# Laying every engine's order of steps anew in a one-core attention and feed-forward kernel

## The reference

```python
x = x + attn(layernorm(x), Wqkv, Wo)      # 16 heads of 32, causal mask, softmax over 512 keys
x = x + ffn(layernorm(x), w1, w3, w2)     # hidden width 1365
# attn: qkv = x @ Wqkv ; a = softmax(q k^T / sqrt(32)) ; o = (a @ v) @ Wo
# ffn:  each weight w is made ternary first: s = mean|w| ; w = clip(round(w / s), -1, 1) * s
#       (silu(x w1^T) * (x w3^T)) @ w2^T
```

## Time and profile before

| | |
|---|---|
| median of 3 runs | 579.03 us (578.77 to 580.35) |
| the profiled execution's own time | 580.78 us |
| its span, first to last instruction | 579.0 us |
| PE, DVE, POOL, ACT busy | 508.0, 411.8, 368.4, 330.2 us |
| mean granted TensorE clock | 0.941 |

### The profile page before, as it was taken

The page is one execution under the profiler, slowest core; times in us unless marked ns, Lnnn a source line. Parts: engine busy times, 40 slices in busy tenths (PEclk is TensorE's granted clock), DMA queues, the critical chain, the costliest instruction groups (busy, mean ns, idle before and its releaser), DMA issues.

```text
span 579.0 us, 11497 instructions
## 1 busy us (share of the span) xinstructions
PE 508.0 (88%) x4092; PEld 237.9 (41%) x4092; DVE 411.8 (71%) x1026; ACT 330.2 (57%) x833; POOL 368.4 (64%) x460
## 2 busy tenths in 40 slices
PE   2669754857999999999999999999999998839997
PEld 2224322333445444544444444454444454314443
DVE  6599787697899877966888879578878771523421
ACT  4769866777756875645467875363666752012320
POOL 3077689777968976776667887556668782312320
PEclk9689955878999999999999999999999999869999
DMA  8939978999889756387596565675783548030001
GB/s 312 316 30 278 193 170 160 252 200 211 153 141 162 145 124 131 56 158 194 108 167 143 90 131 97 141 180 114 101 173 75 109 87 208 9 63 1 0 37 72
DMA packets 224205, 79.52 MB, mean 137 GB/s; under 512 B 213226, under 2 KB 213226, under 8 KB 224148
## 3 DMA queue, kind: packets, MB, share of 16 engines
q1 hardware_dynamic: 224148, 78.79, 65.0%
HBM read 20.97 MB, written 4.19 MB: 43 GB/s over the span
## 4 chain that ended last, share of the span: by engine, by line
PE 69%; POOL 9%; DMA 8%; SPq 5%; DVE 4%; issue 2%; ACT 2%; DVEq 0%; ACTq 0%
PE work L1120 46%; PE work L1280 13%; DMA early<-early 4%; PE work L1239 4%; PE score_bank L1197 4%; POOL early L654 4%; PE work L1210 2%; DMA rows<-in_L_attn_x 2%; POOL late L687 2%; POOL early L687 1%; SPq L517 1%; DVE early L986 1%; DMA w_ternary<-early 1%; POOL rows L669 1%; DMA late<-rows 1%
## 5 line engine op out<-in xcount | busy, mean ns | idle before, releaser
L654 POOL TENSOR_TENSOR early<-early 128x512 f16<-128x512 f32 (+1 forms) x192 | 193.7, 1021 | 40.4 <-DVE early L986 26.5
L762 ACT ACTIVATE early<-early,exp_bias 128x512 f32<-128x512 f32 (+3 forms) x256 | 140.8, 551 | 76.7 <-POOL exp_bias L661 76.5
L1120 PE MATMUL work<-late,w_ternary 128*128 128x512 f16 (+1 forms) x704 | 158.9, 384 | 10.3 <-DMA late<-rows 10.3
L974 DVE CUSTOM_DVE_ANT_0 early<-score_bank,mask,scalars 128x512 f32<-128x512 f32 (+3 forms) x256 | 131.7, 543 | 32.7 <-POOL early L654 20.4
L986 DVE CAST early<-early 128x512 f16<-128x512 f32 (+1 forms) x148 | 99.5, 690 | 18.1 <-ACT early L762 14.7
L1120 PEld LDWEIGHTS work<-late,w_ternary 128*128 128x128 f16 (+1 forms) x704 | 69.2, 101 | 93.9 <-issue 17.9
L1120 PE MATMUL work<-xt,wqkv_hi 128*128 128x512 f16 x256 | 80.7, 398 | 2.9 <-DVE wqkv_lo L936 2.0
L1280 PE MATMUL work<-w_ternary,late 128*128 128x512 f16 (+1 forms) x352 | 77.7, 379 | 0.0
L679 POOL TENSOR_TENSOR late<-late 128x512 f16<-128x512 f32 (+1 forms) x44 | 51.3, 1168 | 40.1 <-ACT late L799 39.4
L792 ACT ACTIVATE late<-work,scalars 128x512 f32<-128x512 f32 (+1 forms) x44 | 30.0, 682 | 53.0 <-DVE late L1027 36.1
L1120 PE MATMUL work<-xt,wqkv_lo 128*128 128x512 f16 x128 | 51.0, 398 | 0.0
(11 more groups left out here) (103 smaller groups left out, 702.4 us busy)
## 6 DMA issues: line engine op xcount, KB each, us to landing
rows<-in_L_attn_x SPq DMA_DIRECT2D x16, 256.0 KB, 3.0
x_res<-in_L_attn_x SPq DMA_DIRECT2D x12, 256.0 KB, 3.2
out_y<-x_res SPq DMA_DIRECT2D x12, 256.0 KB, 2.8
late<-in_L_ffn_w SPq DMA_DIRECT2D x4, 682.5 KB, 5.5
early<-in_L_ffn_w SPq DMA_DIRECT2D x3, 768.0 KB, 12.8
late<-in_L_ffn_w SPq DMA_DIRECT2D x3, 768.0 KB, 6.7
late<-in_L_attn_Wqkv SPq DMA_DIRECT2D x4, 512.0 KB, 7.2
late<-in_L_attn_Wqkv SPq DMA_DIRECT2D x1, 1024.0 KB, 9.8
```

Source lines behind the costliest of these rows:

```text
L654: pool.tensor_tensor(split_view(s, p, 1, h), raw_view(s, p, h), split_view(s, p, 0, h), ALU.subtract).then_inc(low_done, 1)
L762: last = act.activation(piece, piece, ACT.Exp, bias=bias, accum_out=sums[:, s % 2, at:at + 1])
L974: last = dve.tensor_tensor_reduce(raws[n % RAWS][:, off:off + cols], score_bank[h][:, off:off + cols], mask[:, S - cols:S], scalar(exp_sca ...
L1120: last = pe.matmul(bank, lhs, rhs, start=(n == 0), stop=(n == len(terms) - 1))
```

## The change

The five lists of `ORDERS` are replaced by others. The same steps stand in them, none is added or dropped. Some pieces (the second line of a pair is after):

```diff
-sp:   x_load:1,1 res_load:0,2 res_load:0,1 x_load:1,0 weight_turn:w1,0 res_load:0,0 weight_turn:w1,1
+sp:   x_load:1,0 weight_load:w3,0 x_load:1,1 weight_turn:w1,0-2 weight_load:w3,1-3 probs_turn:0,0-2 xt:1,0-1
...
-pool: stats_x:0,0-3 weight_round:w1,0-6 stats_x:1,0 weight_round:w1,7-8 bias:0,0,1 weight_round:w1,9-10 low:0,0,0
+pool: stats_x:0,0-3 stats_x:1,0 weight_round:w1,0-6 bias:0,0,1 weight_round:w1,7 xt:1,0 weight_round:w1,8
+      bias:0,0,3 low:0,0,0-1 weight_round:w1,9-10 bias:0,1,1 low:0,0,2-3 stats_x:1,1 bias:0,1,3 low:0,1,0-2
...
-act:  weight_sum:w1,2 split:2 weight_sum:w1,3 split:3 split:8 split:4 k:0 q:0 weight_ternary:w1,0 split:5
+act:  weight_sum:w1,2 q:0 split:3 weight_sum:w1,3 norm_x:1,0 k:0 split:8 split:4 q:1 weight_ternary:w1,0 xt:1,0
+      weight_ternary:w1,1 split:5 weight_ternary:w1,2 k:1 weight_ternary:w1,3 exp:0,0,0 split:6-7 exp:0,0,1
...
-dve:  max:1,1,0-2 stats_x:1,2 max:1,1,3 high:1,1,0-1 stats_x:1,3 weight_mean:w3 high:1,1,2-3 max:1,2,0-1 values:0
+dve:  high:1,0,0 wo_split high:1,0,1 max:1,1,0 high:1,0,2 max:1,1,1 high:1,0,3 q:2 max:1,1,2 high:1,1,0 max:1,1,3
+      high:1,1,1 stats_x:1,2 max:1,2,0 high:1,1,2 max:1,2,1 high:1,1,3 stats_x:1,3 max:1,2,2 k:2 max:1,2,3
...
-pe:   scores:1,0 k:2 q:3 scores:1,1 inverse:0 weight_mean:w3 values:0 scores:1,2 scores:2,0-1 inverse:1
+pe:   scores:1,0 weight_mean:w3 q:2 inverse:0 q:3 scores:1,1 k:3 values:0 scores:1,2 k:2 scores:2,0-1 inverse:1
```

In code one wait changes. The DMA that turns a tile of the next batch's rows overwrites `xt`. Before, it waited for `q` and `k` of the batch's last slot and for the four `v`. Now it waits, for each of the four banks, for the last `q`, `k` or `v` of the batch that used that bank, which covers all twelve readers:

```diff
                 if kind == "xt":
-                    for used in [(m, GROUPS * b - 1) for m in "qk"] + [("v", b - 1, j) for j in range(ST)]:
-                        full(sp, used)
+                    readers = [(m, GROUPS * (b - 1) + g) for m in "qk" for g in range(GROUPS)]
+                    readers += [("v", b - 1, j) for j in range(ST)]
+                    for n_bank in range(NW):
+                        full(sp, max((r for r in readers if bank_of(r) == n_bank), key=turn_of))
                     sp.wait_ge(rows_split[n], ST * (b - 1) + i + 1)
```

312 lines of the change are left out of this document (159 added, 153 removed).

## The result

The changed kernel takes **611.65 us** (median of 4 runs, 611.0 to 612.59) against 579.69 of the kernel before on the same chip: ratio 1.056, interval 1.054 to 1.058. Slower was forecast, at 593.5 with a range to 605; the time lies outside it. The profiled execution has a span of 610.0 us against 579.0.

A forecast was written before the change was run, and what follows sets the result against it. PE's own work was taken to bound the kernel from 163 us on, softmax waits before it. Waits of +20.5 less 6 recovered gave +14.5: 595.3 profiled, 593.5 median; own range 587 to 600, with rivals 581 to 605.

The forecast's parts named there:

- First part: the x tile: At the start, DVE waits for the x tile behind Wo; q:0 7.8 us later, POOL's first w1 rounding +6.0 us.
- Second part: w3's load ahead of w1's turns: On SP, the w3 load waits for split:7 with w1's turns queued behind; the first fills' turns land +11.1 us later.
- Third part: the wait for all readers: Row turns wait for late k:2, so DVE stands 10.5 us for the third tile; 9.4 of +20.5 us.
- The clock: Idle PE falls to 1.2 GHz, so q:3, k:3 and k:2 take 5.1 us each; sum some 4 us higher.
- Recovery up to 163 us: Up to 163 us, early w3 rounds on POOL and a w3 turn out of the chain give back 6 us.
- The region from 163 us on, put at nothing: From 163 us on, PE's work is unchanged and others have room: no cost, 1 to 3 us if cover fails.
- PE gapless from about 178: Sign expected in the profile after; the sum is wrong if PE's gapless part starts within 5 us of 163.
- The sum: Whole kernel: 20.5 - 6 = +14.5 us, giving 595.3 profiled and 593.5 as median; chance 0.50.
- no recovery: Rival: slots up to 163 us run no tighter than before; +20.5 to 24.5 us, about 601; chance 0.20.

The follow-up runs named there:

- e1: Kernel after with stats_x:1,0 (the wait for the second batch's x tile) moved behind split:2 on DVE; 603.75 us, ratio to before 1.044.
- e2: Kernel after with w3's first load on SP moved between the second and third of w1's turns; 609.45 us, ratio 1.052.
- e3d: e3c plus weight_load:w2,0 ahead of the row turns and the statistics and norms of tiles 1,2 and 1,3 later still; 611.6 us, ratio 1.056.
- e3: Kernel after with k:2 alone moved directly behind q:2 on PE, ACT and DVE; 611.88 us, ratio 1.057.
- f1: Kernel before with all its old lists and only the new condition, row turns waiting for the last reader of every bank; 578.41 us, ratio 0.999.
- e8: Kernel after with the first probability turn of slots 1 and 2 moving only a quarter of its blocks (output not the reference's); 604.88 us, ratio 1.044.
- e5: Kernel after with the four w2 turns behind probs_turn:4,1 and v:1,3's drain ahead of high:5,0,0; 616.15 us, ratio 1.063.
- e5c: Kernel after with only w2's last turn behind probs_turn:4,1, probs_turn:4,2 ahead of the y turns, and v:1,3's drain earlier; 613.01 us, ratio 1.058.
- e6: Kernel after with the edits of e1, e2, e3b and e5 together; 609.14 us, ratio 1.051.
- e7: Kernel after with the edits of e1, e2, e3c and e5c together; 601.16 us, ratio 1.038.
- e10: Kernel after with the edits of e9 and e5c together; 618.3 us, ratio 1.067.
- e11: Kernel after with the edits of e1, e2, e3d, e9 and e5c together; 608.88 us, ratio 1.051.
- e12: Kernel after with w3's turns, the roundings and ternary steps of w2,1 to w2,3, ot:3 and v:1,3's drain earlier; 613.24 us, ratio 1.058.
- e3b: Kernel after with all four late projections of the first batch, with their drains, moved to where the kernel before has them; 614.21 us, ratio 1.060.
- e3c: Kernel after with probs_turn:1,0 ahead of the two row turns on SP, statistics and norms of tiles 1,2 and 1,3 later; 609.16 us, ratio 1.052.
- e9: Kernel after with w3's last rounding and turns, w2's last load, sums, mean, roundings and ternary steps all earlier; 615.45 us, ratio 1.062.
- g1: Kernel before with stats_x:1,0 moved behind k:0 on DVE; 575.37 us, ratio 0.992.

## Why the prediction was wrong, step by step

**First part: the x tile.** Right. `q:0` at 28.2 (forecast 28.8), first rounding at 37.1 (38.3), so +4.8 where +6.0 stood. By e1 the wait is worth 6.8 us at `values:0` and 7.9 in the time, the largest gain of a single reordering.

**Second part: w3's load ahead of w1's turns.** Right in kind. SP was silent until 50.3 (52), and the three turns were issued by 60.0 (third out at 59.1). `high:1,0,0` stood at 81.1 (80.6). By e2 the load's place is worth 3.4 us at `values:0` and 2.2 in the time.

**Third part: the wait for all readers.** The times were right: `k:2` at 93.0 to 95.8 (done 96.0), DVE idle 8.2 us (10.5) up to 101.9 (102.7), `probs_turn:1,0` at 100.9 (101), `high:1,2,0` at 110.0 (109), so +21.4 for the forecast +20.5. What the part is worth by itself was given as 9.4. The stretch `values:0` to `values:1` did lose 9.2, and e3d got 5.3 of it back. The other 4 were not isolated: e3 had nearly as short a stretch (27.5) only because `values:0` itself came 6.3 later. The wait without the lists costs nothing (f1).

**The clock.** The granted clock did fall where PE idled: from 100 to 163 us, with PE busy 34.2 of 63 us, it was 0.70 on average, against 0.88 with 50.2 of 63 before. The Trainium skill, "TensorE: Matmul & The Clock Gate", Part 1, says that an idle array falls to 1.2 GHz; the trace agrees with the rule. The price of 4 us, which I worked out for that rival, was wrong: `q:3`, `k:3` and `k:2` took 2.7 us each, at the high level. `q:2` stood ahead of them (76.6 to 81.3, 4.7 us, for the most part at the low level), PE was busy from 74.7 after 6.9 us of idle time, and from 70 to 100 the mean was 0.82, higher than before's 0.57.

**Recovery up to 163 us.** This step failed. I took -6: 4.2 us for w3's rounds done ahead on POOL and 2.3 for a turn of w3 out of the way, with DVE's 18 us of idle time as the room. Measured from `values:1` to `values:3`: -1.3. The old and the new lists take 45.0 to 46.9 us there in all thirteen kernels whose lists are unchanged from `values:1` to `values:3`. The rounds were done ahead, the sixth at 93.8 us, though by four and not six: by its own `high:1,2,0` at 88.54 the kernel before had started two (84.84 and 87.90). But a round less on POOL shortens nothing unless POOL is what the others wait for, and in the new lists DVE waited 8.4 us there for turned probabilities; e8 shows that shorter turns do shorten the slots. How much of the missing recovery this makes was not isolated. And the turn of w3 was not saved, only moved. SP of the kernel after:

```profile
122.20 3.20 SPq L611 DMA_TRANSPOSE w_ternary<-late  x1
...
165.49 4.20 SPq L611 DMA_TRANSPOSE w_ternary<-late  x2
```

One of the three still stands ahead of `probs_turn:2,0`. The other two stand just ahead of `values:3`, and ACT waited 3.25 us for them at 173.4, with `ot:3` behind it, for which PE idled 1.3 us ahead of `project:0,0`. An engine's idle time in such a stretch is not room until one knows what it waits for.

**The region from 163 us on, put at nothing.** This step failed by more: +10.5 us from `values:3` to `gate:0,0`. I argued that PE has no gaps from 163 on, so that only the point at which this begins could move, and granted 1 to 3 us if the cover failed. But that was a reading of the kernel before; in the new lists the stretch up to `gate:0,0` has gaps of its own (1.3 us ahead of the first projection, 7.7 ahead of `values:4`). "PE gapless from about 178" was the mark set for it, and it is gapless only from 208.6. SP of the kernel before in this place:

```profile
167.69 4.47 SPq L557 DMA_TRANSPOSE late<-rows  x2
172.25 1.92 SPq L568 DMA_TRANSPOSE early<-early  x1
175.25 2.60 SPq L557 DMA_TRANSPOSE late<-rows  x2
```

There the turns of y rows 0 and 1 left in one piece ahead of `probs_turn:4,2`, the second of them 23.7 us behind `values:3`. In the kernel after `probs_turn:4,2` stands between them, behind w2's four turns (8.1 us), and the second leaves at 201.8, 33.5 us behind `values:3`. What hangs on it can be followed in the rows. DVE, kernel after, then PE of e5:

```profile
205.18 1.16 DVE L891 TENSOR_SCALAR rows<-x_res,y_mean_var,y_rstd 128x512 f32<-128x512 f32 x1 [0.45 <-DMA late<-rows]
```

```profile
215.02 10.23 PE L1129 MATMUL work<-late,w_ternary 128*128 128x512 f16 x37 [1.35 <-DMA late<-rows]
```

DVE normalises y row 3 as soon as the turn of y row 1 has landed, ACT halves it by 207.0, its own turn leaves at 208.3 (behind `x_load:2,2` at 206.5 and y row 2's turn) and lands at 211.4, and `gate:0,0` needs it. In the kernel after PE comes to `gate:0,0` 1.2 us later than that, at 212.6, since `values:4` was late as well. So two chains of nearly the same length lead to this step, and mending `values:4` alone could give no more than about 1 us. In e5, e5c, e6, e7, e10, e11 and e12, where `v:1,3` stands earlier, the gate product starts 0.2 us behind the last y turn's landing. So it is shown that the y turns hold it up once `values:4` doesn't. That bringing them forward would give back the 8.2 us is argued: no run did it. In e5c and e12 the second y turn stayed at 201.8 and 202.1, and the gate product at 213 to 214. The edit that would test it is `yt:0,1` ahead of `probs_turn:4,2` with the w2 turns earlier, and w2's loads kept ahead of their sums.

**The sum.** +14.5 forecast, +31.0 in the span. The 16.5 between them are +2.8 in the first three parts, +4.7 from the missing recovery and +10.5 from slot 4, less 1.6 in what follows `gate:0,0`. The two failed steps make 15.2 of it. The rival "no recovery" (601) was nearer than the forecast; it too had nothing for slot 4. The range's upper end of 605 added that rival's size but no cost of its own for the part behind 163, where the text granted at most 3 us.

## What to carry to other kernels

- Cut both kernels at the same steps (here the starts of `values:s` and of `gate:0,0`), not at the same times. One such table showed that what follows `gate:0,0` is constant to 4 us in 400, and where each loss arises. Look whether the same work stands between the marks: here one fill of scores had changed sides.
- A new order is a new set of stalls. A region in which the old order had no gaps tells what work is there, not that another order has none: put a cost on it wherever the lists in it changed too.
- Idle time of an engine is not yet room to catch up. Ask what it waits for before booking a recovery: here DVE waited 8.4 us for turned probabilities, and a transfer booked as out of the way stood further down.
- Moving one step seldom moves one wait: its drains, its loads and the steps queued behind them come along. In e3, e3b, e3c, e5c, e9 and e12 a wait of 3 to 8 us stood in another place. One move paid in both sets of lists, the step that waits for a late tile put behind the steps that don't (e1 and g1).

## What the runs showed of the hardware

- A tile issued behind large transfers comes late: in the kernels before, after and e1, VectorE's wait for the x tile ended at 29.1, 26.3 and 26.5 us. In the kernel after it was issued between 13.1 and 14.7, right behind Wo's 1 MB (issued at 12.0, landed 13.7 us later), so it took 12 to 13 us, where the median of these tiles is 3.3.
- A transposing DMA holds SP's queue the longer the larger it is: 5.4 us for the first fill's turn in slot 2, 1.2 us for a quarter of its blocks. The size isn't all: the same turn in slot 0, issued behind the rest of w3, held SP for 9.0 us (in e1, from 55.96 to the next at 65.0).
